# Low parts of every second score tile on GpSimd, for tiles of one or two key blocks, in a fused attention and ternary feed-forward layer

## The chip, the cores and the metric

The kernel runs on one core of one Trainium2 chip, in one launch. The metric is the device time of one execution in microseconds (us), from the first to the last instruction of that core; lower is better. Engines are named as the profile names them: PE is TensorE, DVE is VectorE, ACT is ScalarE, POOL is GpSimd, SP is SyncE, which here only issues DMAs.

## The reference

The input x is 4 batches of 1024 rows of 512. With xn the layer-normalised x, the output is x plus a causal multi-head attention of xn plus a ternary feed-forward of xn:

```python
c_Q = rms_norm(x @ Wq_down, q_norm_w)                # latent queries, 192 wide
q_nop = c_Q @ Wq_up; q_pe = rope(c_Q @ Wq_pe)        # 16 heads of 128 + 64
c_KV = rms_norm(x @ Wkv_down, kv_norm_w)             # latent keys and values, 128 wide
k_nop, v = split(c_KV @ Wkv_up)                      # 8 key-value heads, each for 2 query heads
k_pe = rope(rms_norm(x @ Wk_pe, k_pe_norm_w))        # one for all heads
scores = einsum(q, k) * (128 + 64) ** -0.5           # causal mask
y = softmax(scores) @ v
attention = y @ Wo
feed_forward = ternary(xn) @ (ternary(weight) + rram_variation).T
out = x + attention + feed_forward
```

## The kernel before

**Precision.** All matmuls run on float16 operands. Where the product must be near float32, an operand is kept as two parts: a high part, the value rounded to float16, and a low part, the rounded remainder. Three products (high times high, high times low, low times high) are summed in PSUM.

**Tiling.** The 4 batches of 1024 rows give 32 row tiles (b, i) of 128 rows, i from 0 to 7, taken in a fixed order `ORDER`: (0,0) to (0,5), (1,0), (0,6), (1,1), (0,7), (1,2) and so on, so that batches overlap. A row tile is worked in four head groups g of four heads h each. `n` counts head groups in that order (128 of them, n = 4t + g for the t-th tile) and `u` = 4n + h counts **score tiles** (512): the scores of 128 rows against the i + 1 key blocks up to the diagonal, so 128(i + 1) columns. The score tiles of heads 0 and 1 leave out 64 columns (`columns(u)`) except near the start and the end. Tiles of one or two key blocks are those with i = 0 or 1.

**One score tile through the engines.** PE computes the scores into PSUM. DVE's `maximum(u)` (line 1524) adds the mask and writes the negated scores into the buffer `P[u % 4]` and the row's extreme into nm. ACT's `exponent(u)` (line 1118) exponentiates P in place and sums the rows. POOL's `scale_sum(u)` (line 1771) scales that sum, DVE's `inverse(u)` (line 1532) takes the reciprocal rc. ACT's `scaled_hi(u)` (line 1113) writes the high part F = P * rc in float16. DVE's `scaled_lo(u)` (line 1538) writes the low part P * rc - F beside it, in one pass:

```python
e.eng.scalar_tensor_tensor(out=m.F[:, slot, at + lo:at + lo + w], in0=m.P[:, u % 4, 0:w],
                           scalar=m.rc[:, u % 8:u % 8 + 1], in1=m.F[:, slot, at:at + w],
                           op0=ALU.mult, op1=ALU.subtract).then_inc(s.fl, 1)
```

For tiles with i up to 1 one transposing DMA on SP (line 1906) then turns both parts of all four heads at once, and PE multiplies them with the values.

**Order of the work.** Each engine has its program written out by hand, in steps (n, p) with p = 0, 1. In step (n, p) the score tiles u = 4(n + 2) + 2p and u + 1 pass through maximum, exponent, scale_sum and inverse, while PE weighs the values of head group n and makes the queries of n + 4. An engine runs its list in order and stands still at a semaphore that is not met. For tiles with i up to 3 the pieces are, in step (n, p):

- DVE: maximum(u), maximum(u + 1), then scaled_lo(u - 2), for p = 0 `rotate` (lines 1333 to 1335), scaled_lo(u - 1), inverse(u), inverse(u + 1), for p = 1 `queries_lo` (line 1341) and `values_lo` (line 1544). In step p = 0 of g = 2 it then has `x_signs` (lines 1273 and 1278), which makes the ternary input XG, XS of a later tile.
- ACT: exponent(u), exponent(u + 1), for p = 1 `rotated_hi` and `queries_hi` (line 982), scaled_hi(u), `values_hi`, scaled_hi(u + 1).
- POOL: scale_sum(u), scale_sum(u + 1), for p = 0 `rotated` (line 1715), for p = 1 `rotated_lo` (line 1721). In g = 1 it also has, at the end of p = 0, `rotate_keys` (lines 1676 to 1680) and, at the end of p = 1, `keys` (lines 1689 to 1692) and `x_lo` (line 1668), 512 columns wide.
- PE: lines 554 and 545 begin `up_pe`, which overwrites the PSUM bank that queries_lo has read; line 829 begins `combine`, which needs values_lo; line 470 begins `down`, which needs the transposed XS.

The semaphore `fl` counts low parts: maximum(u) waits for that of u - 4, since it overwrites the same P buffer, inverse(u) for that of u - 8, and the transposing DMA for that of its last head.

## Time and profile before

| | |
|---|---|
| median of 3 runs | 1683.85 us (1683.62 to 1684.14) |
| the profiled execution | 1683.0 us, of which span 1681.2 us |
| mean granted TensorE clock | 0.996 |
| PE busy | 1643.5 us (98%) |
| DVE busy | 1308.7 us (78%) |
| ACT busy | 1117.2 us (66%) |
| POOL busy | 595.3 us (35%) |

The span is the time between the first and the last instruction in the profile; the execution's own time is 1.8 us longer. Busy time of one engine says nothing of whether it is on the path that sets the end: for that one reads which engine waits for which, and where. Times in the rows below are microseconds from the start of the span unless marked ns. The work with i = 0 and 1 stands at four places: head groups n = 0 to 7 (up to about 145 us), 24 to 27 and 32 to 35 (about 339 to 475 us), and the same pattern for the third and the fourth batch about 400 us and 800 us later.

### The profile page before, as it was taken

To read this page: it belongs to the slowest core of one execution; us is meant where nothing else is said; L and a number is where in the kernel's file an instruction comes from. 1 tells how busy PE (TensorE), PEld (TensorE's weight loads), DVE (VectorE), ACT (ScalarE), POOL (GpSimd) and SP (SyncE) were. 2 spreads that over 40 slices of the span, in tenths; PEclk is the share of its full clock that TensorE was granted. 3 is DMA by queue.
4 is the path that set the end of the run, shared out by engine and by line. 5 is a ranking of instruction groups with operands and counts; after the bars stand their busy time and mean duration, and the time that the engine had idled before them with its cause. 6 is when DMAs were issued, how large, how long until landed. Compare 5 with 4: busy or idle time off the path is not lost.

```text
span 1681.2 us, 34116 instructions
## 1 busy us (share of the span) xinstructions
PE 1643.5 (98%) x11624; PEld 924.3 (55%) x11624; DVE 1308.7 (78%) x3370; ACT 1117.2 (66%) x2464; POOL 595.3 (35%) x1079
## 2 busy tenths in 40 slices
PE   6989999999999999999999999999999999999999
PEld 5655555555555556555554555555555555655544
DVE  6887878778788788778878687877878878877775
ACT  6876766667677576657767576666767767666663
POOL 2433333333333333333333333333333333333330
PEclk8999999999999999999999999999999999999999
DMA  9346776768778677876857877776877857777776
GB/s 263 88 78 118 121 134 132 127 104 149 131 131 153 111 135 134 148 130 107 147 100 148 149 125 135 131 128 104 150 130 131 149 113 138 133 140 130 133 133 123
DMA packets 780264, 221.25 MB, mean 132 GB/s; under 512 B 766968, under 2 KB 769402, under 8 KB 779770
## 3 DMA queue, kind: packets, MB, share of 16 engines
q1 hardware_dynamic: 769392, 195.41, 66.8%
q10 hardware_dynamic: 9162, 17.37, 3.3%
q0 software_dynamic: 1536, 6.29, 1.2%
q8 instruction: 92, 1.51, 0.4%
q14 instruction: 82, 0.67, 0.1%
HBM read 19.76 MB, written 8.39 MB: 17 GB/s over the span
## 4 chain that ended last, share of the span: by engine, by line
PE 86%; issue 5%; DVE 4%; ACT 2%; POOL 2%; DMA 1%; ACTq 0%; DVEq 0%; POOLq 0%; SPq 0%
PE bank L731 7%; PE bank L732 6%; PE bank L734 6%; PE bank L733 6%; PE bank L829 6%; PE bank L831 6%; PE bank L830 6%; PE bank L776 5%; PE bank L777 5%; PE bank L778 5%; PE bank L744 4%; PE bank L485 2%; PE bank L486 2%; PE bank L519 2%; PE bank L524 2%
## 5 line engine op out<-in xcount | busy, mean ns | idle before, releaser
L1118 ACT ACTIVATE P<-P,nm 128x256 f32<-128x256 f32 (+15 forms) x512 | 381.9, 746 | 412.5 <-DVE nm L1524 411.7
L1524 DVE CUSTOM_DVE_ANT_0 P<-bank,mask,neg 128x256 f32<-128x256 f32 (+15 forms) x512 | 383.0, 784 | 246.0 <-PE bank L744 239.1
L1771 POOL TENSOR_SCALAR sn<-sm 128x1 f32<-128x1 f32 x512 | 207.6, 405 | 889.6 <-ACT P L1118 878.7
L1113 ACT ACTIVATE F<-P,rc 128x256 f16<-128x256 f32 (+15 forms) x512 | 365.3, 741 | 101.0 <-DVE rc L1532 65.0
L1538 DVE SCALAR_TENSOR_TENSOR F<-P,rc,F 128x256 f16<-128x256 f32 (+15 forms) x512 | 402.2, 797 | 2.8 <-ACT F L1113 2.4
L732 PE MATMUL bank<-K,Q 128*128 128x512 f16 (+7 forms) x760 | 241.9, 319 | 0.0
L734 PE MATMUL bank<-K,QP 128*128 128x512 f16 (+7 forms) x760 | 241.9, 319 | 0.0
L731 PE MATMUL bank<-K,Q 128*128 128x512 f16 (+7 forms) x760 | 241.8, 319 | 0.0
L733 PE MATMUL bank<-K,Q 128*128 128x512 f16 (+7 forms) x760 | 241.8, 319 | 0.0
L829 PE MATMUL bank<-WO,YH 128*128 128x512 f16 x512 | 194.3, 380 | 5.0 <-DVE YL L1544 4.8
L831 PE MATMUL bank<-WO,YL 128*128 128x512 f16 x512 | 194.1, 379 | 0.0
L830 PE MATMUL bank<-WO,YH 128*128 128x512 f16 x512 | 194.1, 379 | 0.0
L776 PE MATMUL bank<-FT,V 128*128 128x512 f16 x444 | 168.4, 379 | 0.0
L778 PE MATMUL bank<-FT,V 128*128 128x512 f16 x444 | 168.3, 379 | 0.0
L777 PE MATMUL bank<-FT,V 128*128 128x512 f16 x444 | 168.3, 379 | 0.0
L1715 POOL TENSOR_TENSOR R<-R,R 128x256 f32<-128x256 f32 x128 | 146.4, 1144 | 60.6 <-DVE R L1335 59.0
L519 PE MATMUL bank<-C,WM 128*128 128x128 f16 x512 | 112.6, 220 | 0.9 <-DVE Q L1341 0.9
L524 PE MATMUL bank<-C,WM 128*128 128x128 f16 x512 | 112.6, 220 | 0.0
L523 PE MATMUL bank<-C,WM 128*128 128x128 f16 x512 | 112.6, 220 | 0.0
L522 PE MATMUL bank<-C,WM 128*128 128x128 f16 x512 | 112.6, 220 | 0.0
L731 PEld LDWEIGHTS bank<-K,Q 128*128 128x128 f16 x760 | 74.3, 98 | 67.9 <-DVE nm L1524 1.2
L732 PEld LDWEIGHTS bank<-K,Q 128*128 128x128 f16 x760 | 74.3, 98 | 66.3 <-issue 0.3
(228 smaller groups left out, 3234.0 us busy)
## 6 DMA issues: line engine op xcount, KB each, us to landing
out<-X ACTq DMA_DIRECT2D x31, 256.0 KB, 2.8
X<-in_x ACTq DMA_DIRECT2D x28, 256.0 KB, 3.8
FT<-F SPq DMA_TRANSPOSE x348, 4.2
wo<-in_Wo POOLq DMA_DIRECT2D x4, 1024.0 KB, 7.8
V<-CC SPq DMA_DIRECT2D x64, 32.0 KB, 2.5
QP<-QS SPq DMA_TRANSPOSE x128, 2.7
X<-in_x SPq DMA_DIRECT2D x4, 256.0 KB, 6.8
kv<-in_Wkv_up POOLq DMA_DIRECT2D x1, 1024.0 KB, 6.9
```

Source lines behind the costliest of these rows:

```text
L731: e.eng.matmul(o, qh, K[:, AHI, keys], start=True, stop=False)
L732: e.eng.matmul(o, qh, K[:, ALO, keys], start=False, stop=False)
L733: e.eng.matmul(o, ql, K[:, AHI, keys], start=False, stop=False)
L734: e.eng.matmul(o, qp, K[:, BHI, keys], start=False, stop=False)
L776: e.eng.matmul(o, vh, hi, start=start, stop=False)
L829: e.eng.matmul(m.pO, yh, wh, start=(g == 0 and h == 0), stop=False)
L830: e.eng.matmul(m.pO, yh, wl, start=False, stop=False)
L831: op = e.eng.matmul(m.pO, yl, wh, start=False, stop=(g == NG - 1 and h == 3))
L1113: return e.eng.activation(dst, src, ACT.Copy, scale=scale)
L1118: e.eng.activation(m.P[:, u % 4, 0:w], m.P[:, u % 4, 0:w], ACT.Exp, bias=m.nm[:, u % 8:u % 8 + 1], scale=-1.0, accum_out=m.sm[:, u % 8:u % ...
L1524: e.eng.tensor_tensor_reduce(out=m.P[:, u % 4, 0:w], in0=m.pS[u % 2][:, off:off + w], in1=m.mask[:, end - w:end], scale=m.neg[:, :], scala ...
L1538: e.eng.scalar_tensor_tensor(out=m.F[:, slot, at + lo:at + lo + w], in0=m.P[:, u % 4, 0:w], scalar=m.rc[:, u % 8:u % 8 + 1], in1=m.F[:, sl ...
```

## The change

For score tiles of odd u (heads 1 and 3) whose row tile has i up to 1, from u = 8 on, the low part is made on POOL. There are 60 of them: 12 of 64 columns, 16 of 128, 12 of 192 and 20 of 256. DVE's scaled_lo returns at once for them. POOL makes the part in two passes: a tensor_scalar multiplies P by rc in place, and, once a semaphore `pg` says that this is done, a tensor_tensor subtracts F and writes the low part. A new semaphore `fg` counts these low parts, and every wait on `fl` becomes a wait on both counts (`low_parts`). On POOL the two passes for u - 2 and u - 1 (only u - 1 is ever odd) stand at the start of step (n, p), ahead of scale_sum(u).

```diff
--- before.py
+++ after.py
@@ -137,6 +137,23 @@
 def mask_end(u):
 
     return 1088 if side(u) == 0 and whole(u // 4) else 1024
+
+
+def small(u):
+
+    return u % 2 == 1 and u >= 4 * AHEAD and where(u // 4)[1] <= 1
+
+
+SMALL = [0]
+for _u in range(4 * N):
+    SMALL.append(SMALL[-1] + small(_u))
+
+
+def low_parts(e, s, u):
+
+    e.wait_ge(s.fl, u + 1 - SMALL[u + 1])
+    if SMALL[u + 1]:
+        e.wait_ge(s.fg, SMALL[u + 1])
 
 
 def score_cuts(u):
@@ -369,6 +386,7 @@
         self.q_in = sems("q_in", 2)
         self.s, self.mk, self.ex, self.sm, self.rc, self.fh, self.fl = (
             sem("s"), sem("mk"), sem("ex"), sem("sm"), sem("rc"), sem("fh"), sem("fl"))
+        self.fg, self.pg = sem("fg"), sem("pg")
         self.ft_in = sems("ft_in", FSLOTS)
         self.pv, self.yh, self.yl, self.c, self.acc = sem("pv"), sem("yh"), sem("yl"), sem("c"), sem("acc")
 
@@ -1518,7 +1536,7 @@
         off, _ = score_cuts(u)
         e.wait_ge(s.s, u + 1)
         if u >= 4:
-            e.wait_ge(s.fl, u - 3)
+            low_parts(e, s, u - 4)
         if u >= 8:
             e.wait_ge(s.ex, u - 7)
         e.eng.tensor_tensor_reduce(out=m.P[:, u % 4, 0:w], in0=m.pS[u % 2][:, off:off + w], in1=m.mask[:, end - w:end],
@@ -1528,10 +1546,12 @@
     def inverse(u):
         e.wait_ge(s.sm, u + 1)
         if u >= 8:
-            e.wait_ge(s.fl, u - 7)
+            low_parts(e, s, u - 8)
         e.eng.reciprocal(m.rc[:, u % 8:u % 8 + 1], m.sn[:, u % 8:u % 8 + 1]).then_inc(s.rc, 1)
 
     def scaled_lo(u):
+        if small(u):
+            return
         w, lo = columns(u), blocks_wide(u)
         slot, _, at = parts_place(u)
         e.wait_ge(s.fh, u + 1)
@@ -1771,6 +1791,18 @@
         e.eng.tensor_scalar(m.sn[:, u % 8:u % 8 + 1], m.sm[:, u % 8:u % 8 + 1], 2.0 ** -12, None,
                             ALU.mult).then_inc(s.sm, 1)
 
+    def small_lo(u):
+        if not small(u):
+            return
+        w, lo = columns(u), blocks_wide(u)
+        slot, _, at = parts_place(u)
+        e.wait_ge(s.fh, u + 1)
+        e.eng.tensor_scalar(m.P[:, u % 4, 0:w], m.P[:, u % 4, 0:w], m.rc[:, u % 8:u % 8 + 1], None,
+                            ALU.mult).then_inc(s.pg, 1)
+        e.wait_ge(s.pg, SMALL[u + 1])
+        e.eng.tensor_tensor(m.F[:, slot, at + lo:at + lo + w], m.P[:, u % 4, 0:w], m.F[:, slot, at:at + w],
+                            ALU.subtract).then_inc(s.fg, 1)
+
     for u in range(4 * AHEAD):
         scale_sum(u)
     for n in range(N):
@@ -1778,6 +1810,8 @@
         for p in range(2):
             u = 4 * (n + AHEAD) + 2 * p
             if u < 4 * N:
+                small_lo(u - 2)
+                small_lo(u - 1)
                 scale_sum(u)
                 scale_sum(u + 1)
             if n + 2 * AHEAD < N:
@@ -1898,7 +1932,7 @@
         w = 128 * (where(n)[1] + 1)
         at, end = h * 2 * w, end + 2 * w
         e.wait_ge(s.fh, u + 1)
-        e.wait_ge(s.fl, u + 1)
+        low_parts(e, s, u)
         if n == N - 1:
             e.wait_ge(s.up, N)
         elif FT_OVER[n] is not None:
```

On POOL, this is the list from the end of `rotated` in step (1, 0) to `rotated` in step (2, 0), before. TENSOR_SCALAR on sn is scale_sum, TENSOR_TENSOR on QS is rotated_lo, that on XS is x_lo:

```order
L1771 TENSOR_SCALAR sn_118<-sm_117 128x1 [waits rc,ex] x2
L1721 TENSOR_TENSOR QS_76<-R1_77,QS_76 128x2x2x64 [waits ph]
L1689 CAST CC_68<-KR_69 128x128 [waits cl,kp]
L1690 COPY CC_68<-CC_68 128x2x64
L1692 TENSOR_TENSOR CC_68<-KR_69,CC_68 128x128 [waits kh]
L1668 TENSOR_TENSOR XS_63<-XN_62,XS_63 128x512 [waits xh]
L1771 TENSOR_SCALAR sn_118<-sm_117 128x1 [waits rc,ex] x2
L1715 TENSOR_TENSOR R1_77<-R1_77,R2_78 128x256 [waits ropeq]
```

And the same stretch of POOL's list now:

```order
L1800 TENSOR_SCALAR P_71<-P_71,rc_119 128x128 [waits fh]
L1803 TENSOR_TENSOR F_72<-P_71,F_72 128x128 [waits pg]
L1791 TENSOR_SCALAR sn_118<-sm_117 128x1 [waits rc,ex] x2
L1741 TENSOR_TENSOR QS_76<-R1_77,QS_76 128x2x2x64 [waits ph]
L1709 CAST CC_68<-KR_69 128x128 [waits cl,kp]
L1710 COPY CC_68<-CC_68 128x2x64
L1712 TENSOR_TENSOR CC_68<-KR_69,CC_68 128x128 [waits kh]
L1688 TENSOR_TENSOR XS_63<-XN_62,XS_63 128x512 [waits xh]
L1800 TENSOR_SCALAR P_71<-P_71,rc_119 128x128 [waits fh]
L1803 TENSOR_TENSOR F_72<-P_71,F_72 128x128 [waits pg]
L1791 TENSOR_SCALAR sn_118<-sm_117 128x1 [waits rc,ex] x2
L1735 TENSOR_TENSOR R1_77<-R1_77,R2_78 128x256 [waits ropeq]
```

Two passes stand ahead of each pair of scale_sum; the second pair of passes comes between x_lo and scale_sum.

On DVE, step (2, 0) before, from maximum(17)'s end to x_signs (lines 1333 to 1335 are rotate):

```order
L1538 SCALAR_TENSOR_TENSOR F_72<-P_71,rc_119,F_72 128x128 [waits fh]
L1333 TENSOR_TENSOR R1_77<-bank3,rope_50 128x256 [waits pl,upe]
L1334 TENSOR_TENSOR R2_78<-bank3,rope_50 128x4x32
L1335 TENSOR_TENSOR R2_78<-bank3,rope_50 128x4x32
L1538 SCALAR_TENSOR_TENSOR F_72<-P_71,rc_119,F_72 128x128 [waits fh]
L1532 RECIPROCAL rc_119<-sn_118 128x1 [waits sm] x2
L1273 TENSOR_SCALAR XG_64<-XN_62 128x512 [waits xq,xn]
L1278 SCALAR_TENSOR_TENSOR XS_63<-XN_62,XG_64 128x512 [waits xt_in,xg]
```

And now:

```order
L1558 SCALAR_TENSOR_TENSOR F_72<-P_71,rc_119,F_72 128x128 [waits fh]
L1351 TENSOR_TENSOR R1_77<-bank3,rope_50 128x256 [waits pl,upe]
L1352 TENSOR_TENSOR R2_78<-bank3,rope_50 128x4x32
L1353 TENSOR_TENSOR R2_78<-bank3,rope_50 128x4x32
L1550 RECIPROCAL rc_119<-sn_118 128x1 [waits sm] x2
L1291 TENSOR_SCALAR XG_64<-XN_62 128x512 [waits xq,xn]
L1296 SCALAR_TENSOR_TENSOR XS_63<-XN_62,XG_64 128x512 [waits xt_in,xg]
```

The second low part is gone, so rotate is followed by the reciprocals, which wait for POOL's scale_sum. PE, ACT and SP keep their lists; only semaphores of SP's transposing DMA differ.

## Rows read from the trace of the kernel before

**Rows 1.** The page: busy time of each engine over the whole span.

```profile
PE 1643.5 (98%) x11624; PEld 924.3 (55%) x11624; DVE 1308.7 (78%) x3370; ACT 1117.2 (66%) x2464; POOL 595.3 (35%) x1079
```

**Rows 2.** Waits of TensorE from 84 to 154 us: total, times, longest.

```profile
PE bank L554 <- DVE Q L1341: 3.3, 3, 1.2
PE bank L545 <- DVE Q L1341: 0.6, 1, 0.6
```

**Rows 3.** Waits of TensorE from 310 to 480 us, the second batch's small tiles.

```profile
PE bank L829 <- DVE YL L1544: 1.6, 4, 0.6
PE bank L554 <- DVE Q L1341: 0.6, 1, 0.6
```

**Rows 4.** VectorE's groups by shape, line 1538: busy us, mean ns, idle before.

```profile
L1538 DVE SCALAR_TENSOR_TENSOR F<-P,rc,F 128x256 f16<-128x256 f32 x40 | 19.2, 489 | 0.0
L1538 DVE SCALAR_TENSOR_TENSOR F<-P,rc,F 128x128 f16<-128x128 f32 x40 | 14.0, 354 | 0.0
L1538 DVE SCALAR_TENSOR_TENSOR F<-P,rc,F 128x192 f16<-128x192 f32 x24 | 8.9, 411 | 0.0
```

**Rows 5.** GpSimd's groups by shape.

```profile
L1715 POOL TENSOR_TENSOR R<-R,R 128x256 f32<-128x256 f32 x128 | 146.4, 1144 | 60.6 <-DVE R L1335 59.0
L1704 POOL COPY K<-KT 128x512 f16<-128x512 f16 x32 | 20.5, 641 | 0.0
L1692 POOL TENSOR_TENSOR CC<-KR,CC 128x128 f16<-128x128 f32 x32 | 13.7, 427 | 0.0
L1689 POOL CAST CC<-KR 128x128 f16<-128x128 f32 x32 | 10.1, 316 | 0.1
```

**Rows 6.** GpSimd in order of time: start us, us, instruction, idle before.

```profile
101.69 0.25 POOL L1678 TENSOR_TENSOR KR<-KR,rope 128x32 f32<-128x32 f32 x1
102.02 0.32 POOL L1680 TENSOR_TENSOR KR<-KR 128x64 f32<-128x64 f32 x1
106.99 1.16 POOL L1668 TENSOR_TENSOR XS<-XN,XS 128x512 f16<-128x512 f32 x1 [1.47 <-ACT XS L904]
108.23 0.50 POOL L1771 TENSOR_SCALAR sn<-sm 128x1 f32<-128x1 f32 x2
108.81 0.73 POOL L1715 TENSOR_TENSOR R<-R,R 128x256 f32<-128x256 f32 x1
```

**Rows 7.** VectorE in order of time, the same stretch.

```profile
99.67 0.34 DVE L1538 SCALAR_TENSOR_TENSOR F<-P,rc,F 128x128 f16<-128x128 f32 x1
104.42 0.69 DVE L1341 TENSOR_TENSOR Q<-bank,Q 128x512 f16<-128x512 f32 x1 [0.33 <-ACT Q L982]
107.48 0.82 DVE L1538 SCALAR_TENSOR_TENSOR F<-P,rc,F 128x128 f16<-128x128 f32 x1
108.48 0.45 DVE L1532 RECIPROCAL rc<-sn 128x1 f32<-128x1 f32 x2 [0.18 <-POOL sn L1771]
108.85 0.97 DVE L1273 TENSOR_SCALAR XG<-XN 128x512 f16<-128x512 f32 x1
```

**Rows 8.** GpSimd in order of time, four head groups later.

```profile
142.51 1.16 POOL L1668 TENSOR_TENSOR XS<-XN,XS 128x512 f16<-128x512 f32 x1 [1.69 <-ACT XS L904]
143.75 0.56 POOL L1771 TENSOR_SCALAR sn<-sm 128x1 f32<-128x1 f32 x2
```

**Rows 9.** VectorE in order of time, four head groups later.

```profile
144.06 0.45 DVE L1532 RECIPROCAL rc<-sn 128x1 f32<-128x1 f32 x2
144.43 0.97 DVE L1273 TENSOR_SCALAR XG<-XN 128x512 f16<-128x512 f32 x1
```

**Rows 10.** GpSimd in the second batch, behind tile (1, 0)'s last head.

```profile
374.44 1.16 POOL L1668 TENSOR_TENSOR XS<-XN,XS 128x512 f16<-128x512 f32 x1 [1.47 <-ACT XS L904]
377.10 0.21 POOL L1771 TENSOR_SCALAR sn<-sm 128x1 f32<-128x1 f32 x1 [1.51 <-ACT P L1118]
```

**Rows 11.** GpSimd in the second batch, behind tile (1, 1)'s last head.

```profile
473.05 1.15 POOL L1668 TENSOR_TENSOR XS<-XN,XS 128x512 f16<-128x512 f32 x1 [1.69 <-ACT XS L904]
475.75 0.30 POOL L1771 TENSOR_SCALAR sn<-sm 128x1 f32<-128x1 f32 x1 [1.55 <-ACT P L1118]
```

## The prediction

> **What bounds the kernel now.** I read the page first. TensorE is busy for 98% of the span, VectorE for 1308.7 us, GpSimd for 595.3 us [rows 1]. So an edit that leaves TensorE's list alone can gain no more than TensorE's idle time, and only that part of it which depends on the edited work. The view of TensorE's waits, cut to the stretches in which the small tiles pass, gives this part. From 84 to 154 us TensorE waits for `queries_lo` 3.3 us in three waits at line 554, and 0.6 us at line 545 [rows 2]. In the second batch's small tiles, 310 to 480 us, the waits are 1.6 and 0.6 us [rows 3], and the same two rows stand in the third and fourth batch. All of it is 3.9 + 3 x 2.2 = 10.5 us, 0.6% of the time. That is the ceiling of any gain. A measurement of this kernel can tell about 0.2%, 3.4 us, from no change.
>
> Next: is the removed work what these waits wait for? In order of time, `queries_lo` at 104.42 us started when ScalarE delivered, after VectorE had stood idle for 0.33 us [rows 7]. ScalarE makes the query's high part after its two exponents and before the scaled high parts, so neither a low part nor a reciprocal of the same step is ahead of it. Only a low part removed in the step before, p = 0, can bring `maximum`, the exponents and then the queries forward, and only where VectorE has no idle time in between.
>
> **What is removed.** The group of low parts by shape gives 489 ns for 256 columns, 411 for 192 and 354 for 128 [rows 4]; 64 columns cost no more than 128. With 20, 12 and 28 of them, VectorE loses at most 20 x 0.489 + 12 x 0.411 + 28 x 0.354 = 24.6 us of work, over 60 places.
>
> **What is added.** GpSimd had neither pass. The first has one float32 tensor and a column of scalars as its inputs. Nearest are a cast of 128 columns, 316 ns, and a copy of 512 columns, 641 ns [rows 5]. A line through them gives 0.42 us at 256 columns and 0.32 at 128. The second pass is a subtraction with a float16 result, as the 128-column one of 427 ns [rows 5] and the 512-column one of 1.16 us [rows 6]; a line through them gives 0.67 us at 256. Between two dependent instructions GpSimd takes 0.08 us (line 1678 ends at 101.94, line 1680 starts at 102.02 [rows 6]). A pair then costs 0.42 + 0.08 + 0.67 = 1.17 us at 256 columns and 0.32 + 0.08 + 0.43 = 0.83 us at 128; 1.00 and 0.65 for 192 and 64 by the same lines. In all GpSimd gets 20 x 1.17 + 12 x 1.00 + 16 x 0.83 + 12 x 0.65 = 56.5 us more, and its 595 us become about 650. The lower bound is a pair that hides wholly. The upper bound is a pass at GpSimd's dearest row for 256 columns, line 1715 with a mean of 1144 ns [rows 5] although it can take 0.73 [rows 6]: 2 x 1.14 + 0.08 = 2.4 us. I take 1.17, since the passes have the shapes of the cheaper rows and run where VectorE's own instructions are short.
>
> **What stands behind the pair.** GpSimd runs in order, and behind the pair stands `scale_sum`, for which `inverse` on VectorE waits. The pair's own wait costs nothing: ScalarE writes the high part of u - 1 before it starts exponent(u). So it matters whether GpSimd is free between that high part and the end of the exponent. In most steps it is. The exceptions are the steps in which `x_lo` runs late.
>
> Step (2, 0), first batch. `x_lo` ends at 106.99 + 1.16 = 108.15 us and the two `scale_sum` start at 108.23 with no idle time before them; the reciprocals at 108.48 wait for them and XG follows at 108.85 [rows 6, 7]. The 128-column pair now comes in between: +0.83 us for the reciprocals, XG, XS, the next maximum, and through exponent and query for line 554, one of the three that TensorE already waits at. Against this, the low part removed at 99.67 us (0.34 us long [rows 7], 0.26 to the next start) brings this whole stretch forward by about 0.26 us, since VectorE is without idle time from there to the next maximum. Leaving out the low part at 107.48 brings nothing: it ends at 108.30, before the reciprocals' start. XS has two inputs in SBUF and meets the next pair's first pass; I add 0.2 us for that. Term: 0.83 - 0.26 + 0.2 = **+0.8 us**.
>
> Step (6, 0), first batch. `x_lo` ends at 142.51 + 1.16 = 143.67 us and `scale_sum` follows at 143.75 [rows 8]; the reciprocals start at 144.06, XG at 144.43 [rows 9], without idle time up to the query, and TensorE waits for it at line 545 already, for 0.6 us [rows 2]. A 256-column pair in between is **+1.2 us**. Nothing is subtracted: TensorE sets the pace of the steps ahead, so earlier low parts gain only idle time there.
>
> The same steps of the later batches. After `x_lo` ends at 375.60 and at 474.20 us, GpSimd idles 1.51 and 1.55 us before `scale_sum` [rows 10, 11], since the next tile is wide and its exponents long. Pairs of 0.83 and 1.17 us fit. Term: 0, and likewise in the third and fourth batch.
>
> In the other steps a pair can push `scale_sum` by up to 0.4 us. VectorE has a low part and `rotate`, or a wait for the query, ahead of the point where this would be felt: term 0. If that cover is gone, each is worth 0.1 to 0.4 us. The transposing DMA starts up to 1 us earlier or 0.7 us later and TensorE has a step to spare for it: term 0. The P buffer is freed before maximum(u + 4), since the next reciprocals, which VectorE has behind it, already stand after the pair: no new wait.
>
> **Sum.** +0.8 + 1.2 = +2.0 us. The profiled execution took 1683.0 us (span 1681.2), which gives 1685.0; the median of the runs lies 0.85 us higher, so for it 1683.85 + 2.0 = **1685.8 us**, +0.12%, within what counts as no change.
>
> The Trainium skill, GPSIMD Engine Reference, section 4.1 Engine selection, speaks against this change: element-wise work with two inputs belongs on VectorE, being about 2x slower on GpSimd, and one-input work runs at about line rate. By that rule a pair of 256 columns would be an estimated 2 x 0.49 + 0.49 + 0.08 = 1.55 us, and the sum about +2.8 us instead of +2.0. The rows here agree in direction: 427 ns for the subtraction of 128 columns alone [rows 5], against 354 ns for VectorE's whole low part [rows 4].
>
> **Rivals.**
>
> *The relief counts and the delay does not* (0.20). VectorE's run of work is what TensorE waits for in the first batch, and without the low parts `x_lo` runs freely and earlier. For it: the low part at 107.48 us took 0.82 us, not 0.34, while `x_lo` ran [rows 6, 7]. Price: 0.26 us off at each of the three waits of line 554, 0.8 us: 1683.1 us, no change. Against: `scale_sum` stands behind the pair in the list and had no idle time in front of it.
>
> *Collisions* (0.08). That low part of 0.82 us shows that a GpSimd instruction and a VectorE one with two SBUF inputs hold each other up by 0.48 us. If each of the pair's passes does so wherever VectorE is without idle time (two steps in each of the four stretches, eight in all, of which four reach TensorE), it is 4 x 0.48 = 1.9 us on top: 1687.7 us, a slowdown just over the limit. The Trainium skill, SBUF - State Buffer, section Who interferes with whom, states that the engines' shared port pair is locked for a whole instruction and the second one blocks fully, also for a VectorE instruction with two SBUF inputs against a GpSimd one that reads. The 0.48 us agree with blocking, and this rival is what the rule would give if every collision counted.
>
> *The pair is slow* (0.07), the case that ends slower. If a pass costs what line 1715 costs on average, the pair is 2.4 us at 256 columns and some 1.6 at 128. Step (6, 0) then loses 2.4, step (2, 0) 1.6 - 0.3 + 0.2 = 1.5. Step (5, 1), where GpSimd comes from `rotate_keys`, loses 1.0, and step (1, 1) 0.5. Sum +5.4: 1689.3 us. It decides from about 1.8 us for 256 columns on.
>
> *A real gain* (0.03). The relief takes half of the ceiling of 10.5 us: 1683.85 - 5.2 = 1678.6 us. Against it is the idle time in front of `queries_lo` [rows 7].
>
> **How the numbers follow.** The forecast has 0.62. The collisions' case, 1687.7, lies at the limit of 1683.85 x 1.002 = 1687.2, so half of it counts on each side. No change: 0.62 + 0.20 + 0.04 = 0.86. Slower: 0.04 + 0.07 = 0.11. Faster: 0.03. The range goes from the relief's case less the 0.2 us by which the runs spread, 1682.9, to the collisions' case and the near part of the slow pair, 1688.3. It leaves out the slow pair's far end and the real gain.
>
> **What would show it.** Right: GpSimd about 650 us busy, with passes of 0.4 and 0.7 us at 256 columns; VectorE about 24 us less busy; in the first batch line 554's waits longer by some 0.6 us and line 545's near 1.8 us instead of 0.6; the waits of the later batches as before. XG of step (2, 0) starts some 0.6 us later, XG of step (6, 0) some 2 us later, both counted from the start. Wrong: the first pass takes over 1 us at 256 columns; line 545 waits as before; new waits of TensorE on VectorE appear near 340 to 475 us; or the waits at line 554 vanish.

## The result: 4.7 us slower, and the profile after

| | before | after |
|---|---|---|
| median of 7 runs | 1683.62 us | 1688.34 us |
| lowest to highest | 1681.96 to 1684.14 | 1687.25 to 1690.02 |
| ratio, 95% interval | | 1.0033 (1.0024 to 1.0042) |
| the profiled execution (span) | 1683.0 (1681.2) | 1687.25 (1685.5) |

The medians differ by 4.7 us, which is 0.28%; the ratio that goes with the interval is 1.0033, 5.6 us, and its interval, 4.0 to 7.1 us, holds both. The kernel is slower by more than the 0.2% that the prediction called its limit. The forecast was no change, +2.0 us, with a range up to 1688.3: the measured time lies at its very edge, just outside, and on the side of slower. One execution of experiment 9's kernel took 1897 us at a mean granted clock of 0.85, a state that no other execution here was in, and is left out of its ratio. Line numbers of after are 18 to 20 higher than in the rows of before: 1558 is scaled_lo, 1550 inverse, 1542 maximum, 1359 queries_lo, 1351 to 1353 rotate, 1317 to 1322 parts_lo, 1688 x_lo, 1791 scale_sum; 1800 and 1803 are the two passes. On TensorE 572 and 563 answer to 554 and 545, 749 starts the scores, 527 starts the half of the query product that overwrites what rotate has read.

The page of after, busy time of each engine, against [rows 1]:

```profile
PE 1646.2 (98%) x11624; PEld 926.5 (55%) x11624; DVE 1299.1 (77%) x3310; ACT 1117.4 (66%) x2464; POOL 668.2 (40%) x1199
```

GpSimd is 73 us busier, where 56.5 were forecast, and VectorE only 9.6 us less busy, where 24 were. Sixty VectorE instructions have gone and 120 have come on GpSimd, so the change does what it says, at another price. Two things make up VectorE's shortfall. Busy time counts the overlap of neighbouring instructions once (0.34 us long, but 0.26 to the next start [rows 7]), so in experiment 7, where GpSimd's work is almost nothing, it falls by 16.6 us and not by 24. The other 7 us are instructions that take longer beside the passes.

GpSimd's groups by shape in after (busy us, mean ns, idle before) give that price:

```profile
L1800 POOL TENSOR_SCALAR P<-P,rc 128x256 f32<-128x256 f32 x20 | 19.6, 978 | 21.3 <-ACT F L1131 21.3
L1800 POOL TENSOR_SCALAR P<-P,rc 128x128 f32<-128x128 f32 x16 | 9.9, 621 | 15.2 <-ACT F L1131 15.2
...
L1803 POOL TENSOR_TENSOR F<-P,F 128x256 f16<-128x256 f32 x20 | 14.1, 706 | 1.7
L1803 POOL TENSOR_TENSOR F<-P,F 128x128 f16<-128x128 f32 x16 | 6.9, 434 | 1.3
```

The second pass is as forecast, 0.71 and 0.43 us against 0.67 and 0.43. The first pass is about twice the forecast: 0.98 us against 0.42 at 256 columns, 0.62 against 0.32 at 128.

VectorE's group by shape for the low parts of 256 columns that stayed with it, in after; 489 ns before [rows 4]:

```profile
L1558 DVE SCALAR_TENSOR_TENSOR F<-P,rc,F 128x256 f16<-128x256 f32 x20 | 11.5, 573 | 0.0
```

They take 84 ns more each, 1.7 us in all, and that is part of what VectorE did not save: they now run beside a pass of the neighbouring score tile.

Waits of TensorE from 84 to 154 us in after (total, times, longest), against [rows 2]:

```profile
PE bank L572 <- DVE Q L1359: 3.7, 3, 1.4
PE bank L749 <- DVE nm L1542: 1.5, 2, 1.0
...
PE bank L563 <- DVE Q L1359: 0.5, 1, 0.5
...
PE bank L527 <- DVE R L1353: 0.2, 1, 0.2
```

The old wait at the query is 0.4 us longer, and TensorE now also waits for `maximum`, 1.5 us. A further 1.3 us at line 563 falls at 154.6 us, just behind this window. The same view from 310 to 480 us, against [rows 3]:

```profile
PE bank L847 <- DVE YL L1564: 1.6, 4, 0.6
PE bank L572 <- DVE Q L1359: 0.6, 1, 0.6
PE bank L527 <- DVE R L1353: 0.6, 2, 0.4
```

The two old rows are unchanged; the third is new, and it returns in the third and fourth batch. The prediction had named new waits of TensorE on VectorE here as a sign that it was wrong.

**Where along the span the time is lost.** The table takes the start of line 576, a product of `up_pe`, for head group n, and subtracts the start of the same product in a control in which the test for small tiles always fails (its experiment is below). All are set to zero at n = 1, ahead of the first changed instruction, since the start-up alone differs by up to 4.3 us between profiled executions (n = 1 is reached between 48.9 and 53.2 us). Values are us; up_pe of group n runs in the steps of n - 4.

| n | 5 | 7 | 10 | 11 | 12 | 16 | 38 | 70 | 102 | 127 |
|---|---|---|---|---|---|---|---|---|---|---|
| after | 0.33 | 1.69 | 2.08 | 3.40 | 2.56 | 2.57 | 3.22 | 3.90 | 4.04 | 4.04 |

The delay comes in steps: +0.33 behind step (0,1), +1.26 behind (2,0), about +0.5 behind (5,1) (from 1.60 at n = 9), +1.3 behind (6,0), 3.4 us in all. From n = 16 on it grows in each later batch, by another 1.5 us. That is the net growth: it comes in six jumps of 0.33 to 0.34 us (two in each batch, the first two ahead of n = 30 and n = 38), 2.0 us together. Between them it falls at n = 68, 96 and 100, by 0.65 us together, and it falls by as much at the same places in experiment 10's kernel, which has none of the jumps; so this part is the control's execution, and the jumps are worth 2.0 us. The fall of 0.8 between them isn't the change's: near 160 us TensorE has a wait at line 805, with no releaser that the profile shows, of 1.2 us in the control's execution, 0.7 in that of before, 0.5 in this one, and 0.4 to 1.0 in those of experiments 2, 3 and 7, delayed or not.

One profile for each kernel is a weak measure where no wait with a name stands behind a step. The kernel before has the same instructions as the control, and by this table it is 0.9 us ahead of the control at n = 12, then 1.0 us behind it at n = 16 (a wait of 1.7 us for the transposed XS at 194 us, which the control does not have there), and 1.1 us behind at the end. So I use the steps that have a wait behind them, and not the last entry.

**Step (2,0), the forecast's +0.8.** GpSimd in after, in order of time (start us, us, instruction, idle before), against [rows 6]:

```profile
108.77 1.16 POOL L1688 TENSOR_TENSOR XS<-XN,XS 128x512 f16<-128x512 f32 x1 [1.28 <-ACT XS L922]
109.91 0.62 POOL L1800 TENSOR_SCALAR P<-P,rc 128x128 f32<-128x128 f32 x1
110.61 0.43 POOL L1803 TENSOR_TENSOR F<-P,F 128x128 f16<-128x128 f32 x1
111.12 0.51 POOL L1791 TENSOR_SCALAR sn<-sm 128x1 f32<-128x1 f32 x2
```

and VectorE and TensorE in after, against [rows 7]:

```profile
111.38 0.45 DVE L1550 RECIPROCAL rc<-sn 128x1 f32<-128x1 f32 x2 [2.04 <-POOL sn L1791]
111.74 0.97 DVE L1291 TENSOR_SCALAR XG<-XN 128x512 f16<-128x512 f32 x1
112.75 0.85 DVE L1296 SCALAR_TENSOR_TENSOR XS<-XN,XG 128x512 f16<-128x512 f32 x1
```
```profile
114.15 0.27 PE L749 MATMUL bank<-K,Q 128*128 128x256 f16 x1 [1.03 <-DVE nm L1542]
```

The pair stands between x_lo and scale_sum as forecast, but takes 111.12 - 109.91 = 1.21 us from its start to scale_sum's. The forecast's 0.83 ends with the second pass; counted so, the pair is 0.62 + 0.08 + 0.43 = 1.13 us. VectorE, without its low part, is idle 2.04 us for it. XS takes 0.85 us beside the next pair's first pass, 0.69 in the control: a meeting worth 0.16 us, where I had added 0.2. With n = 1 set to zero, x_lo starts 0.43 us later than in the control and scale_sum 1.54 us later (the control's start at 108.87 and 110.11). So the pair adds 1.11 us here, the meeting 0.16, and the 0.26 us that I had subtracted for the low part that is gone do not appear.

**Step (6,0), the forecast's +1.2**, GpSimd and then VectorE in after, against [rows 8, 9]:

```profile
147.05 0.94 POOL L1800 TENSOR_SCALAR P<-P,rc 128x256 f32<-128x256 f32 x1
148.07 0.67 POOL L1803 TENSOR_TENSOR F<-P,F 128x256 f16<-128x256 f32 x1
148.82 0.50 POOL L1791 TENSOR_SCALAR sn<-sm 128x1 f32<-128x1 f32 x2
```
```profile
149.07 0.45 DVE L1550 RECIPROCAL rc<-sn 128x1 f32<-128x1 f32 x2 [2.30 <-POOL sn L1791]
```

Here the pair takes 1.77 us to scale_sum's start, 1.69 to its own end, instead of 1.17. The steps (5,1) and (6,0) are not two losses. x_lo waits for ScalarE, and with n = 1 set to zero it starts 1.5 us later than in the control (145.66 here, 144.66 there), no more than the 1.6 us of n = 9: the late query of (5,1) has not reached it. Both steps together, from 1.60 to 3.39, cost 1.8 us, about the length of the one pair behind x_lo.

**Step (0,1), a term 0 of the forecast.** GpSimd and VectorE in after:

```profile
96.14 0.62 POOL L1800 TENSOR_SCALAR P<-P,rc 128x128 f32<-128x128 f32 x1 [1.22 <-ACT F L1131]
96.85 0.43 POOL L1803 TENSOR_TENSOR F<-P,F 128x128 f16<-128x128 f32 x1
97.36 0.49 POOL L1791 TENSOR_SCALAR sn<-sm 128x1 f32<-128x1 f32 x2
```
```profile
97.60 0.45 DVE L1550 RECIPROCAL rc<-sn 128x1 f32<-128x1 f32 x2 [0.90 <-POOL sn L1791]
97.97 0.67 DVE L1359 TENSOR_TENSOR Q<-bank,Q 128x512 f16<-128x512 f32 x1
```

In the control, as before, the query stands behind an idle time of 0.33 us for ScalarE. Now there is none: the reciprocals are so late that the query waits for them. The cover that the prediction named is gone. Counted from this step's first maximum (95.14 here, 95.67 in the control) the query starts 0.35 us later (2.83 against 2.48), all of which reaches TensorE.

**Step (25,0), a later batch.** GpSimd and VectorE in after, then TensorE:

```profile
368.81 0.62 POOL L1800 TENSOR_SCALAR P<-P,rc 128x128 f32<-128x128 f32 x1 [1.82 <-ACT F L1131]
369.52 0.43 POOL L1803 TENSOR_TENSOR F<-P,F 128x128 f16<-128x128 f32 x1
```
```profile
368.89 0.37 DVE L1317 SCALAR_TENSOR_TENSOR KR<-CR,RM,nwk 128x64 f32<-128x64 f32 x1
...
369.51 0.58 DVE L1322 SCALAR_TENSOR_TENSOR CC<-CR,RM,CC 128x128 f16<-128x128 f32 x1
```
```profile
371.55 0.23 PE L527 MATMUL bank<-C,WM 64*128 64x128 f16 x1 [0.41 <-DVE R L1353]
```

The same two VectorE instructions in the control:

```profile
366.85 0.27 DVE L1317 SCALAR_TENSOR_TENSOR KR<-CR,RM,nwk 128x64 f32<-128x64 f32 x1
...
367.37 0.35 DVE L1322 SCALAR_TENSOR_TENSOR CC<-CR,RM,CC 128x128 f16<-128x128 f32 x1
```

GpSimd has time to spare here. But `parts_lo` reads two tensors in SBUF and two of its three instructions each meet a pass: 0.37 and 0.58 us instead of 0.27 and 0.35. That puts rotate 0.3 us back, and TensorE waits for rotate at line 527, where it had never waited before.

### The profile page after: what moved, and what is told of

Same layout as the page of the kernel before. It is cut to its first block, busy times and chain, and to the rows that moved or that the text cites. A ratio compares the mean times of both kernels' runs of the same rounds, so it can differ in the third digit from the quotient of the medians.

```text
span 1685.5 us, 34179 instructions
## 1 busy us (share of the span) xinstructions
PE 1646.2 (98%) x11624; PEld 926.5 (55%) x11624; DVE 1299.1 (77%) x3310; ACT 1117.4 (66%) x2464; POOL 668.2 (40%) x1199
## 4 chain that ended last, share of the span: by engine, by line
PE 85%; issue 5%; DVE 5%; ACT 2%; POOL 2%; DMA 1%; DVEq 0%; ACTq 0%; POOLq 0%; SPq 0%
PE bank L749 6%; PE bank L752 6%; PE bank L750 6%; PE bank L751 6%; PE bank L847 6%; PE bank L849 6%; PE bank L848 6%; PE bank L794 5%; PE bank L795 5%; PE bank L796 5%; PE bank L762 4%; PE bank L503 2%; PE bank L504 2%; PE bank L537 1%; PE bank L542 1%
## 5 line engine op out<-in xcount | busy, mean ns | idle before, releaser
L1558 DVE SCALAR_TENSOR_TENSOR F<-P,rc,F 128x320 f16<-128x320 f32 (+10 forms) x452 | 383.1, 855 | 2.8 <-ACT F L1131 2.4
L1550 DVE RECIPROCAL rc<-sn 128x1 f32<-128x1 f32 x512 | 77.2, 158 | 58.1 <-POOL sn L1791 38.0
L749 PEld LDWEIGHTS bank<-K,Q 128*128 128x128 f16 x760 | 74.4, 98 | 70.6 <-issue 3.0
```

The source lines that it names most:

```text
L749: e.eng.matmul(o, qh, K[:, AHI, keys], start=True, stop=False)
```

## The experiments

Theory A: the pair stands ahead of scale_sum in steps where GpSimd has no idle time, and its length there is the loss. Theory B: VectorE and GpSimd hold each other up where their instructions meet; some expectations let it grow with the number of pairs. Besides these, the relief of VectorE could be worth something and hide part of either. The expectations of experiments 1 and 4 name a theory C: that part of the loss is the later start-up of the profiled execution (n = 1 at 50.3 us in after, 48.9 in before). Each ratio is against the kernel before on the same chip, with its 95% interval; the median of before was 1682.73 us for the first four, 1683.33 for the next four and 1682.99 for the last three.

**1. Nothing is moved: a control.** The code stays, but as no tile counts as small, nothing waits for the new semaphores.

```diff
-    return u % 2 == 1 and u >= 4 * AHEAD and where(u // 4)[1] <= 1
+    return False
```

> No tile counts as small: the instructions of before with the line numbers of after. Every theory: 1683.6 us. Its profile shows how far the stretch before the first changed instruction (the start of the attention, TensorE's query product near 48.9 us in before and 50.3 us in after) moves from execution to execution: if by 1 us or more, theory C has its 1.3 us from that; if it stays within 0.3 us of before, the 1.3 us need a cause in the change.

1683.33 us, 1.0002 (0.9993 to 1.0011). The code around the change costs nothing that can be measured; this profile is the base of the table above. It reaches n = 1 at 50.8 us with the instructions of before, so the late start of after's profile needs no cause in the change. It does not explain the loss either, which is one of medians.

**2. Only the first batch.** 12 pairs.

```diff
-    return u % 2 == 1 and u >= 4 * AHEAD and where(u // 4)[1] <= 1
+    return u % 2 == 1 and u >= 4 * AHEAD and where(u // 4)[1] <= 1 and u < 32
```

> Only the 12 pairs of the first batch (u below 32) are on GpSimd. By the profile of after, the first batch's steps lose 3.7 us and 1.9 us of it is given back at the transposed XS near 195 us. Theory A: net +1.8 us against before, 1685.4 us. If the giving back is not tied to the change: +3.7 us, 1687.3. Theory B would spread the loss by the number of pairs, 12 of 60: +0.9 us, 1684.5 us.

1686.72 us, 1.0021 (1.0012 to 1.0030).

**3. Only the later batches.** 48 pairs.

```diff
-    return u % 2 == 1 and u >= 4 * AHEAD and where(u // 4)[1] <= 1
+    return u % 2 == 1 and u >= 4 * AHEAD and where(u // 4)[1] <= 1 and u >= 32
```

> Only the 48 pairs of batches two to four are on GpSimd. In the profile of after they showed two new waits of TensorE at line 527 in each batch, 0.4 and 0.2 us, from collisions with VectorE's instructions with two SBUF inputs. Theory A: scale_sum's delay costs nothing here and the collisions 3 x 0.6 = 1.8 us: 1685.4 us. Theory B: 48 of 60 of the loss, +3.7 us, 1687.3 us. My prediction's term for these batches was 0: 1683.6 us.

1685.21 us, 1.0013 (1.0005 to 1.0022). The loss has two parts, +4.0 and +2.5 us by the medians. Those add up to more than 4.7; the ratios, 0.0021 and 0.0013, add up to the change's 0.0033. By the table's measure the two profiles read:

| n | 5 | 7 | 10 | 11 | 12 | 16 | 38 | 70 | 102 | 127 |
|---|---|---|---|---|---|---|---|---|---|---|
| first batch only | 0.35 | 1.73 | 2.20 | 3.54 | 3.25 | 3.25 | 3.27 | 3.53 | 3.05 | 3.06 |
| later batches only | 0.02 | 0.03 | -0.24 | -0.24 | -1.00 | -1.00 | -0.33 | 0.30 | 0.51 | 0.52 |

The first stops growing when its pairs end. The second grows by 1.5 us net from n = 16 on, some 0.34 at a time; the -1.00 ahead of that is mostly the wait at line 805 again, in an execution that had nothing late there. Four fifths of the pairs make the smaller part of the loss, so the loss sits in places and is not spread evenly over the pairs.

**4. The pair behind the two scale_sum.** If A holds alone, the loss should go.

```diff
-                small_lo(u - 2)
-                small_lo(u - 1)
                 scale_sum(u)
                 scale_sum(u + 1)
+                small_lo(u - 2)
+                small_lo(u - 1)
```

> The pair of passes stands behind the two scale_sum of its step instead of ahead of them; same instructions. Theory A (the loss comes from scale_sum, and with it the reciprocals, standing behind the pair): most of the +4.7 us goes, about 1684.5 us, the reciprocals of step (2, 0) wait for about 0.2 us instead of 2.0, and the new waits of TensorE at lines 749 and the wait at line 563 near 154 us return to those of before. Theory B (collisions of the two passes with VectorE on SBUF, wherever they stand): the loss stays, 1688 us. Theory C (the profile of after was already 1.3 us late before the first changed instruction, so part of the loss is not the change's): about 1685.5 us, and a prologue as late as in after.

1698.77 us, 1.0095 (1.0081 to 1.0109), from four executions: a miss by 14 us. VectorE did get its sums earlier (its reciprocals in step (2,0) wait 0.93 us instead of 2.04, where I had expected 0.2). But head 3's low part is now ready later, and SP issues its DMAs in order. SP's queue in this kernel:

```profile
112.83 1.23 SPq L1940 DMA_TRANSPOSE FT<-F  x1
114.25 1.44 SPq L1850 DMA_TRANSPOSE XT<-XS  x1
```

and in the control:

```profile
110.25 1.23 SPq L1940 DMA_TRANSPOSE FT<-F  x1
112.57 1.42 SPq L1850 DMA_TRANSPOSE XT<-XS  x1
```

The transpose of F is issued 2.6 us later, and behind it in the queue that of XS 1.7 us later (0.24 us of each is the difference at n = 1). TensorE's waits over the whole span in this kernel:

```profile
PE bank L488 <- DMA XT<-XS: 6.7, 3, 3.8
...
PE bank L805 <- DMA FT<-F: 3.0, 3, 1.7
```

These waits, 9.7 us, are not the whole of 16. Behind the longest of them TensorE runs slower. The stretches 118 to 124 and 162 to 168 us in this kernel, then the first of them in the control (the third number from the end is the granted clock):

```profile
core 0: us, PE busy (x) PEld busy (x) DVE busy (x) ACT busy (x) POOL busy (x), PEclk, DMA share, GB/s
118.00:124.00 6.00, 3.88 (x13) 1.89 (x14) 0.24 (x3) 0.91 (x2) 2.30 (x3) 0.50 0.97 140
162.00:168.00 6.00, 4.87 (x15) 2.20 (x16) 0.87 (x5) 1.01 (x2) 1.02 (x1) 0.50 0.80 124
```
```profile
118.00:124.00 6.00, 6.00 (x55) 3.84 (x54) 3.05 (x13) 3.37 (x10) 2.28 (x5) 1.00 0.84 100
```

In both stretches the granted clock is 0.50, the lower of its two levels, 1.2 GHz instead of 2.4. It falls while TensorE stands idle for XT, and is back at 1.00 at 125 and at 169 us, TensorE having been busy again from 120.1 and 163.1 us on. The twelve products behind the first wait take 3.79 us from the first start to that of line 847, and 1.95 in the control:

```profile
120.12 0.48 PE L488 MATMUL bank<-wdh,XT 128*128 128x384 f16 x1 [3.82 <-DMA XT<-XS]
...
123.91 0.63 PE L847 MATMUL bank<-WO,YH 128*128 128x512 f16 x1
```
```profile
116.48 0.32 PE L488 MATMUL bank<-wdh,XT 128*128 128x384 f16 x1 [0.23 <-DMA XT<-XS]
...
118.43 0.38 PE L847 MATMUL bank<-WO,YH 128*128 128x512 f16 x1
```

Half of TensorE's busy time in the two stretches, (3.88 + 4.87) / 2 = 4.4 us, is an estimate of what the low clock costs here. The change itself has no such stretch behind its start-up.

So the place that the change chose is the better of the two, and the low part of a group's last head may not be late.

**5. Head 1 alone, behind the two scale_sum.** If experiment 4 failed through head 3 and SP, the same order is harmless for head 1: its part is needed a whole step earlier than the transpose.

```diff
-    return u % 2 == 1 and u >= 4 * AHEAD and where(u // 4)[1] <= 1
+    return u % 4 == 1 and u >= 4 * AHEAD and where(u // 4)[1] <= 1
```

with the order of experiment 4.

> Only the low parts of head 1 (30 of the 60) are on GpSimd, and their pair stands behind the two scale_sum of its step p = 1; head 3 stays on VectorE. The transposing DMA waits for all four heads only in the next step, so these low parts are not urgent. From the run with all pairs behind scale_sum (+16 us) I read that the late low part of head 3 holds SP's queue: the transposing DMA of the probabilities was issued 2.6 us later, those of XS and the keys stand behind it. Theory SP: here the loss vanishes, 0 to +0.7 us against before. If instead every pair behind scale_sum costs (the rotated_lo and x_lo behind it): half of 16 us, +8 us.

1683.14 us, 0.9998 (0.9989 to 1.0006). Thirty pairs cost nothing that can be measured, and gain nothing. So the cause in experiment 4 is with the low part of head 3; that it acts through SP's queue is read from the profile above and was not tried by itself.

**6. The two pairs behind x_lo stay on VectorE**, those of steps (2,0) and (6,0).

```diff
-    return u % 2 == 1 and u >= 4 * AHEAD and where(u // 4)[1] <= 1
+    return u % 2 == 1 and u >= 4 * AHEAD and where(u // 4)[1] <= 1 and u not in (15, 31)
```

> As the change, but the two pairs that stand right behind x_lo in the first batch, of u = 15 in step (2, 0) and u = 31 in step (6, 0), are left on VectorE; 58 pairs remain on GpSimd. In the profile of after the pair put 1.21 us (128 columns) and 1.77 us (256 columns) between x_lo and scale_sum. Theory A (the loss is the pair standing ahead of scale_sum where GpSimd has no idle time): about 2.5 to 3.0 us of the change's 4.7 us go, +1.7 to +2.2 us over before, about 1685 us. Theory B (collisions and crowding by the number of pairs): 58 of 60 of the loss stay, +4.5 us.

1685.06 us, 1.0015 (1.0007 to 1.0024), against 1.0033 for the change. These two of the sixty pairs carry somewhat more than half of the loss: 0.0018 of 0.0033 by the ratios, 3.0 of 4.7 us by the medians. The rest is not explained by them: the prediction had put the whole sum there. By the table's measure this profile has 0.33 at n = 5, 0.43 at n = 9, 0.91 at n = 10 and 0.63 at n = 11. The step behind (0,1) stays, and of the 0.5 behind (5,1) only 0.2 is left once no pair stands behind x_lo in (6,0).

**7. A memset of zeros in place of both passes.** The kernel leaves out these 60 low parts. The relief of VectorE remains, with only 0.32 us on GpSimd for 256 columns.

```diff
-        e.eng.tensor_scalar(m.P[:, u % 4, 0:w], m.P[:, u % 4, 0:w], m.rc[:, u % 8:u % 8 + 1], None,
-                            ALU.mult).then_inc(s.pg, 1)
-        e.wait_ge(s.pg, SMALL[u + 1])
-        e.eng.tensor_tensor(m.F[:, slot, at + lo:at + lo + w], m.P[:, u % 4, 0:w], m.F[:, slot, at:at + w],
-                            ALU.subtract).then_inc(s.fg, 1)
+        e.eng.memset(m.F[:, slot, at + lo:at + lo + w], 0.0).then_inc(s.fg, 1)
```

> As the change, but in place of the two passes GpSimd writes zeros to the low part with one memset, which reads nothing; the low parts of these 60 score tiles are left out of the result. VectorE stays relieved as in the change. Theory A: with a pair of some 0.2 us nothing is lost, and what VectorE's relief is worth shows: 0 to -1 us against before (0.26 us at each wait of line 554 that TensorE has in the first batch). Rival D (the loss lies in the changed waits and lists, or in VectorE's changed pace, not in the length of the passes): +3 us or more stay.

1682.69 us, 0.9996 (0.9987 to 1.0005). With an almost free replacement the relief is worth 0.6 us, within the interval of nothing, and by the same interval not more than 2.2 us. So no price of the passes would have made this change pay by more than that. The loss goes with the passes, although the lists, the new semaphores and VectorE's relief stay as in the change: the expectation's rival D falls.

**8. The second pass alone.** The factor rc is left out of these low parts. The pair becomes one pass, 0.67 us at 256 columns and 0.43 at 128, below what I had forecast for both.

```diff
-        e.eng.tensor_scalar(m.P[:, u % 4, 0:w], m.P[:, u % 4, 0:w], m.rc[:, u % 8:u % 8 + 1], None,
-                            ALU.mult).then_inc(s.pg, 1)
-        e.wait_ge(s.pg, SMALL[u + 1])
```

> As the change, but without the first pass: GpSimd subtracts the high part from the unscaled P, so the factor rc is left out of the low parts of these 60 score tiles. A pair of 1.77 us at 256 columns becomes one pass of about 0.75 us (1.21 to 0.5 us at 128). My mistake in the prediction was the price of the first pass, 0.94 us against 0.42. Theory A: the loss falls with the length, to about 0.4 of 4.7 us, +1.5 to +2 us. Theory B with collisions of the subtracting pass, which reads two inputs: most stays, +3 us or more.

1684.97 us, 1.0013 (1.0004 to 1.0022). The first pass makes about 1.0033 - 1.0013 = 0.0020, 3.4 us, of the loss, by two ratios that are each uncertain by 0.0009, so that the difference is known only to about 2 us. In this kernel TensorE still waits for rotate at line 527, 1.5 us in seven waits over the span; the change has 1.9 us in seven. So most of those waits do not come from the first pass. In the first batch it makes a good third of the loss by the table's measure: 0.01 instead of 0.33 at n = 5 (the query of (0,1) is covered again), and 2.14 instead of 3.39 at n = 11, of which 0.4 stand behind a wait for the transposed F at 126 us that the change does not have.

**9. The passes in all but the places found.** By now the places were: (0,1), (2,0), (5,1) and (6,0) in the first batch, by length, and the step in every batch where the pair meets parts_lo.

```diff
-    return u % 2 == 1 and u >= 4 * AHEAD and where(u // 4)[1] <= 1
+    return u % 2 == 1 and u >= 4 * AHEAD and where(u // 4)[1] <= 1 and u not in (9, 15, 29, 31) and u % 16 != 11
```

> As the change, but 12 of the 60 pairs are left on VectorE: in the first batch those of u = 9 in step (0, 1), 15 in (2, 0), 29 in (5, 1) and 31 in (6, 0), where GpSimd reaches scale_sum late, and in all batches the head 3 of each third head group (u = 11, 27, 107, 139, 235, 267, 363, 395), whose pair meets the two-input instructions of parts_lo on VectorE in step (1, 0) and its like. 48 pairs stay. Theory A with the collisions at one known place: nothing of the loss is left, 0 us against before within 0.7 us, and the waits at line 527 and 749 are gone. Theory B (loss by number): 48 of 60, +3.8 us.

1683.63 us, 1.0003 (0.9994 to 1.0013). 48 of the 60 pairs are still on GpSimd, and no loss can be told from none. TensorE's waits from 310 to 480 us in this kernel:

```profile
PE bank L847 <- DVE YL L1564: 1.6, 4, 0.6
PE bank L572 <- DVE Q L1359: 0.6, 1, 0.6
```

These are [rows 3] again.

**10. The later batches without the step that meets parts_lo.** Experiment 3 less six pairs.

```diff
-    return u % 2 == 1 and u >= 4 * AHEAD and where(u // 4)[1] <= 1
+    return u % 2 == 1 and u >= 4 * AHEAD and where(u // 4)[1] <= 1 and u >= 32 and u % 16 != 11
```

> Only batches two to four, without the six pairs that meet parts_lo (u = 107, 139, 235, 267, 363, 395): 42 pairs. The run with all 48 of these batches gave +2.5 us against before and +1.9 against the same instructions' control. Collision theory: the waits at line 527 (0.6 us in each batch) vanish, and the loss with them: 0 us within 0.7. Otherwise +1.7 us or more stay.

1683.10 us, 0.9997 (0.9989 to 1.0006), where experiment 3 had 1.0013 (1.0005 to 1.0022). Six of 48 pairs carry the later batches' loss, and the wait at line 527 is gone with them.

**11. The first pass times a constant.** Is it the column of scalars that makes the first pass dear? It multiplies by 1.0 instead of rc, so the factor is left out of these low parts.

```diff
-        e.eng.tensor_scalar(m.P[:, u % 4, 0:w], m.P[:, u % 4, 0:w], m.rc[:, u % 8:u % 8 + 1], None,
+        e.eng.tensor_scalar(m.P[:, u % 4, 0:w], m.P[:, u % 4, 0:w], 1.0, None,
```

> As the change, but the first pass multiplies P by the constant 1 instead of by the column rc (the factor is left out of these low parts). It asks why the first pass took 0.94 us at 256 columns where I had 0.42. If reading a scalar for each partition costs it: about 0.4 to 0.5 us at 256 columns. If the float32 output or the pass's own rate does: 0.9 us as in the change.

1686.45 us, a single execution, whose time decides nothing. GpSimd's groups by shape:

```profile
L1800 POOL TENSOR_SCALAR P<-P 128x256 f32<-128x256 f32 x20 | 17.4, 870 | 21.1 <-ACT F L1131 20.8
...
L1800 POOL TENSOR_SCALAR P<-P 128x128 f32<-128x128 f32 x16 | 8.8, 549 | 15.1 <-ACT F L1131 15.1
```

The column of scalars costs 0.11 us at 256 columns (978 against 870) and 0.07 at 128. The rest is the pass itself: 321 ns for 128 further columns, 2.5 ns each. What in it is dear, the multiplication, the float32 result or writing in place, was not tried.

## Why the prediction was wrong

Point by point, by its own steps.

- **The ceiling of any gain** held, and by far: the relief is worth 0.6 us by the medians and at most 2.2 us by the interval, against 10.5 (experiment 7). The reason given, idle time of VectorE ahead of the query, fits that.
- **VectorE loses 24.6 us.** The instructions have gone, but busy time fell by 9.6. About 8 us of the difference is there in experiment 7 too, which saves 16.6, and is mostly how I counted (overlaps counted twice; 64 columns take 277 ns before, not 354); about 7 us are meetings with the passes (for one, 573 against 489 ns at 256 columns).
- **The price of a pair** is the step that failed, in the term of the first pass. I drew a line through a cast of 316 ns and a copy of 641 ns [rows 5], both with float16 results, and got 0.42 us; float32 to float32, times a column, is 0.94 to 0.98. A pair is 1.69 us instead of 1.17 at 256 columns and 1.13 instead of 0.83 at 128, and scale_sum starts another 0.08 behind it, which I had left out. The upper bound of 2.4 us held it; the sum used the low value.
- **Step (2,0)**: right mechanism, +1.26 instead of +0.8. The pair adds 1.11 instead of 0.83 and the meeting 0.16 instead of 0.2. The 0.26 that I took off for the earlier low part is not there: x_lo starts no earlier, and with the passes all but gone, in experiment 7, the table's measure shows -0.08 at n = 6 and +0.06 at n = 7.
- **Step (6,0)**: right mechanism, and the near number, +1.3 for +1.2, is luck. The pair is 0.5 us longer than forecast, and the 0.5 us behind (5,1) is part of the same delay: 1.8 us together, for a term of 1.2.
- **"In the other steps ... term 0. If that cover is gone, each is worth 0.1 to 0.4 us."** It was gone at (0,1), +0.33, and at (5,1), about +0.5. At the forecast price both would have been all but covered: the pair is 0.30 and 0.52 us longer than forecast at these two places, against queries that start 0.35 and 0.55 us late. In experiment 8, whose single pass is shorter than the forecast pair, both queries wait for ScalarE again. So this too follows from the size of the first pass. What (5,1) costs of its own is small, 0.2 us in experiment 6, since (6,0) stands behind it.
- **The later batches, term 0**: the second step that failed. The two steps I looked at, behind x_lo, do have room for the pair, as [rows 10, 11] said. I had not looked at what VectorE does while the pair runs in the others. In one step of each small tile of a batch it runs parts_lo, delayed by 0.3 us, and TensorE waits: six jumps of 0.3 us, 2.0 us in all (1.5 net by the table), and nothing that can be measured once six pairs are taken out (experiments 3, 10). A cheaper first pass would have helped little here, as experiment 8 still has 1.5 us of waits at line 527.
- **The transposing DMA and the P buffer, nothing**: right for the order chosen. Experiment 4 shows how near the limit that is.

Added up by the table: the forecast's 2.0, +0.5 for (2,0), +0.6 for (5,1) and (6,0) together, +0.3 for (0,1), +2.0 for the meetings, makes 5.4 us. The medians differ by 4.7, the ratio says 5.6. (The table's last entry is 4.04, since the control's own longer wait at line 805 and its other delays are in it.) A closer account can't be had from single profiles: two executions of the same instructions, before's and the control's, differ by 1.1 us in this measure, and the ratio's interval is 4.0 to 7.1 us. Of the signs named, the waits at the query came nearly as forecast (line 572 +0.4 us for +0.6, line 563 1.8 us with the wait at 154.6 us), while XG, start-up taken out, came 1.6 and 3.7 us later than before in (2,0) and (6,0), where 0.6 and 2 were forecast.

Of the rivals, *the relief counts and the delay does not* and *a real gain* are out by experiment 7. *The pair is slow* was half true: about 1.7 us for 256 columns lies just under its point of decision, 1.8. Of the uncovered steps that it named, (5,1) and (1,1), the first was found; the other that was found is (0,1). *Collisions* was the mechanism of the later batches. It counted 0.48 us for each of four places; measured are 0.1 to 0.24 us per instruction and 0.33 to 0.34 us per place, at six places. Each rival was given a small chance by itself, both happened in part, and the range had no room for both.

The Trainium skill, GPSIMD Engine Reference, section 4.1 Engine selection, was right to speak against the change, and the estimate worked out from it was nearer than mine, but by errors that cancel in part. (The prediction gives it as +2.8 us; by its own terms, 1.14 - 0.26 + 0.2 + 1.55, it is +2.6.) Its rule gives one-input work at about line rate, an estimated 0.49 us for the first pass where 0.98 was measured, and about twice VectorE's time for two-input work, 0.98 where the subtraction took 0.71. In this trace the one-input float32 pass is the dearer of the two.

## What to carry to other kernels

Work moved to an engine with low busy time costs its whole length wherever that engine has no idle time just ahead of something that others wait for; count those places, price them with the dearest plausible row and not with the nearest shape of another type, and look at what the other engines run in the same microseconds. Removing work from an engine that is not waited for at that point gains little or nothing: a nearly free replacement, such as a memset, shows that ceiling in one run. Where an in-order DMA queue takes the result, lateness of one operand delays the unrelated transfers behind it. And a wait of TensorE can cost more than its length, since the granted clock can be lower behind it: read it too.

## What the runs showed of the hardware

- GpSimd's tensor_scalar in place on float32 takes 0.62 us for 128 columns and 0.98 for 256, 0.55 and 0.87 with a constant as the scalar. The subtraction of two tensors with a float16 result takes 0.43 and 0.71: two inputs were cheaper than one. Whether the type of the result makes this was not tried.
- A GpSimd pass and a VectorE instruction with two tensors in SBUF can hold each other up, and how far depends on the pass. Beside GpSimd's passes with two tensors, the VectorE instruction ends shortly after the pass does, wherever it began. In after:

```profile
139.20 0.76 POOL L1735 TENSOR_TENSOR R<-R,R 128x256 f32<-128x256 f32 x1 [0.36 <-DVE R L1353]
```
```profile
139.40 0.58 DVE L1263 TENSOR_TENSOR SM<-SM 128x1 f32<-128x1 f32 x1
```

  The pass ends at 139.96 us and this small instruction, 0.16 us where it is shortest, at 139.98. parts_lo's third instruction ends 0.14 us after the subtraction of 0.43 us that it meets (370.09 against 369.95 at (25,0)). The Trainium skill, SBUF - State Buffer, section Who interferes with whom, states that the ports which the two engines share are an exclusive lock for a whole instruction, and that the other one blocks; these rows agree. Beside the multiplication, which has one tensor, they do not: parts_lo's first instruction starts inside the pass, at 368.89, grows by only 0.1 us and ends at 369.26, while the pass runs until 369.43.
- In experiment 4 a transposing DMA was issued 2.3 us late (start-up taken out) behind a late low part. TensorE then waited up to 3.8 us for the transfer behind it in the queue, ran at a granted clock of 0.50 for some 6 us twice, and the kernel was 16 us slower.
